# Attention scores as float32r pairs in the two halves of the TensorE array, head outputs kept transposed and collected by DMA, and convolutions of the un-normalised residual sum

## What is computed

```python
x = x + _L0_conv_ref(_gn(x), ...)   # attention, 8 heads of 16 channels
x = x + _L1_conv_ref(_gn(x), ...)   # 7x7 depthwise convolution, layer norm, MLP
# _gn: group norm, 32 groups of 4 channels, over all pixels
# attention, per image and head g (W and b per head, 16x16):
q, k, v = W x + b;  attn = softmax(q.T k * 16**-0.5);  out = v attn.T;  out = Wp out + bp
# second block:
y = conv7x7_depthwise(x) + conv_b
y = (y - mean_c(y)) * rsqrt(var_c(y) + 1e-6) * ln_g + ln_b
y = gelu(y w1 + b1) w2 + b2         # hidden width 512
```

## Time and profile before

| | |
|---|---|
| median of 3 runs | 368.73 us (368.45 to 372.86) |
| the profiled execution | 367.55 us, its span 365.6 us |
| PE busy | 309.8 us (85%) |
| DVE busy | 258.9 us (71%) |
| ACT busy | 194.1 us (53%) |
| POOL busy | 103.9 us (28%) |
| mean granted TensorE clock | 0.925 of full speed |

### The profile page before, as it was taken

The page is one execution under the profiler, slowest core; times in us unless marked ns, Lnnn a source line. Parts: engine busy times, 40 slices in busy tenths (PEclk is TensorE's granted clock), DMA queues, the critical chain, the costliest instruction groups (busy, mean ns, idle before and its releaser), DMA issues.

```text
span 365.6 us, 5601 instructions
## 1 busy us (share of the span) xinstructions
PE 309.8 (85%) x2046; PEld 106.8 (29%) x2046; DVE 258.9 (71%) x270; ACT 194.1 (53%) x359; POOL 103.9 (28%) x137
## 2 busy tenths in 40 slices
PE   7568779999990599999989999998981999698796
PEld 2244123333320133333323333333220344222242
DVE  3746759898970177887748988879898146999820
ACT  1406347767760267767757666766760546453132
POOL 5000051111010011011000036999980100894410
PEclk9969699999995599999999999999995799969899
DMA  5168950000699300000000000590000001960001
GB/s 198 29 210 129 162 104 3 30 31 0 125 120 125 37 1 2 1 2 3 1 2 0 2 2 3 158 204 5 1 2 0 0 0 74 192 167 2 0 0 57
DMA packets 11022, 19.97 MB, mean 55 GB/s; under 512 B 2035, under 2 KB 2931, under 8 KB 10995
## 3 DMA queue, kind: packets, MB, share of 16 engines
q1 hardware_dynamic: 10998, 19.64, 26.6%
HBM read 13.61 MB, written 5.54 MB: 52 GB/s over the span
## 4 chain that ended last, share of the span: by engine, by line
PE 59%; DVE 20%; DMA 9%; issue 4%; SPq 3%; ACT 2%; POOL 2%; DVEq 0%; ACTq 0%; POOLq 0%
PE ps L971 15%; PE ps L930 15%; PE ps L960 12%; DVE qs L744 11%; DMA qs<-mrows 6%; PE ps L1122 4%; DVE mx L696 4%; DMA ks<-parts_dram 2%; PE ps L1136 2%; SPq L331 2%; PE ps L951 2%; PE ps L1081 2%; PE ps L876 2%; PE ps L902 1%; ACT pr L568 1%
## 5 line engine op out<-in xcount | busy, mean ns | idle before, releaser
L696 DVE TENSOR_REDUCE mx<-ps 128x1 f32<-128x1024 f32 x128 | 154.3, 1221 | 55.5 <-PE ps L930 51.0
L568 ACT ACTIVATE pr<-ps 128x512 f32<-128x512 f32 x256 | 139.0, 595 | 98.8 <-PE ps L960 98.7
L960 PE MATMUL ps<-qs,ks 99*128 99x512 bf16 x256 | 79.6, 389 | 17.8 <-DMA qs<-mrows 16.9
L930 PE MATMUL ps<-ks,qs 96*128 96x512 bf16 x256 | 79.4, 395 | 10.7 <-DMA ks<-part 5.5
L971 PE MATMUL ps<-pr,va 128*32 128x256 f32 x1024 | 83.5, 398 | 0.0
L744 DVE SCALAR_TENSOR_TENSOR qs<-xpad,w,qs 128x512 f32<-128x512 f32 (+1 forms) x35 | 54.7, 1562 | 1.0
L433 POOL TENSOR_TENSOR mparts<-zeros,mx 128x8 bf16<-128x8 f32 x16 | 3.7, 230 | 169.0 <-DVE mx L696 169.0
L960 PEld LDWEIGHTS ps<-qs,ks 99*128 99x128 bf16 x256 | 24.5, 99 | 61.2 <-DMA qs<-mrows 16.7
L971 PEld LDWEIGHTS ps<-pr,va 128*32 128x32 f32 x1024 | 20.3, 109 | 51.4 <-issue 46.8
L930 PEld LDWEIGHTS ps<-ks,qs 96*128 96x128 bf16 x256 | 17.0, 99 | 55.5 <-issue 44.2
L1056 PE MATMUL ps<-xr,wt 128*32 128x512 f32 x224 | 30.0, 664 | 3.5 <-DMA xr<-pad_dram 3.5
...
## 6 DMA issues: line engine op xcount, KB each, us to landing
...
```

The costliest lines, as they stand in the source:

```text
L568: nc.scalar.activation(pr[:, j % PR, c * HALF:(c + 1) * HALF], st[c], ACT.Exp, scale=SCALE).then_inc(exp_done, 1)
L696: nc.vector.tensor_reduce(mx[:, r, i:i + 1], sm[i % 2], AX.X, ALU.max).then_inc(max_done, 1)
L930: last = nc.tensor.matmul(sm[i % 2][:, c * HALF:(c + 1) * HALF], qs[0:STACK, bass.ds(s * N + i * P, P)], ks[0:STACK, bass.ds(s * N + c * H ...
L960: nc.tensor.matmul(st[c], ks[0:ROWS, bass.ds(t * N + j * P, P)], qs[0:ROWS, bass.ds(t * N + c * HALF, HALF)], start=True, stop=True).then_ ...
```

## The change

Five things change together.

1. **Scores in float32r.** q and k are kept in `hl` as a float32r part and the rest (PARTS = 2), and a stack has three products: 3 x 16 = 48 rows, or 50 with the maxima. A stack lies in rows 0 to 49 or 64 to 113 of `qs` and `ks`, by heads in turn (`rows_of`: heads 0, 1, 4, 5, 8, 9, 12, 13 below, the others above), so that a score matmul uses half the rows of the array (the built program gives each a tile of 64 x 128). `qs` and `ks` have three cells of 1024 columns, which are reused; `stack` fills one head with six DMAs of 16 partitions x 1024, SBUF to SBUF, three to four heads ahead, behind that head's `row_max` in SP's queue. Nothing of the attention goes through DRAM.
2. **Order and banks.** The transposed scores, the turned maxima and denominators and some small results share the banks 4, 5 and 7 in rotation (`uses_of_banks`, `free`). `both_scores` puts one matmul of `scores_t` and one of `scores` in turn. `times_v` comes for two tiles at a time.
3. **Outputs stay transposed.** `denominators` spreads the sums over the partitions with one matmul (128 x 256), ACT copies that (`copy_turned`), and DVE takes a reciprocal of 128 x 256 and multiplies 128 x 256 (`normalise`). `collect` puts a head's output in `oc` with four DMAs. There is no turning back after heads 7 and 15; head 15 is projected from `on` with a weight of its own (`wlast`).
4. **Convolution before the norm.** `xpad` holds x1 itself (image 0's is copied by POOL, `pad_image`; image 1's is written by `residual_padded`, which replaces L837 and L298). The taps run over it, and `conv_sum` scales the sum by the group's 1/deviation and adds a `border` term, the shift times the sum of the taps inside the image, which POOL builds in `taps_inside`.
5. **Shares of the taps.** Image 0: PE 25 (7 runs), DVE 12, POOL 12. Image 1: PE 32 (9 runs), DVE 17, none on POOL or ACT. Image 1's `xr` is filled from `xpad` directly with 2 x 16 DMAs (`fill_directly`). PE's `keep_busy` matmuls before the first scores grow from 4 to 27, with eight more between the first scores, and the six behind `mlp_down(0)` are gone.

The core of the diff:

```diff
-PARTS = 3
-STACK = 6 * D
+PARTS = 2
+TERMS = 3
+STACK = TERMS * D
 ROWS = STACK + PARTS
-
-Q_ORDER = (0, 1, 2, 0, 1, 0)
-K_ORDER = (0, 0, 0, 1, 1, 2)
+GROUP_ROWS = 64
+CELLS = 3
+
+Q_ORDER = (0, 0, 1)
+K_ORDER = (0, 1, 0)
...
-PE_RUNS = (6, 8)
-DVE_TAPS = (14, 12)
+PE_RUNS = (7, 9)
+DVE_TAPS = (12, 17)
 PE_TAPS = tuple(n // SPAN * KS + n % SPAN * SHIFTS for n in PE_RUNS)
 PE_ROWS = tuple(-(-n // SPAN) for n in PE_RUNS)
-ALONE = 8
-POOL_TAPS = tuple(KS * KS - PE_TAPS[b] - DVE_TAPS[b] for b in range(B))
...
+AHEAD = 2 * NT - 3
+LATER = 2
+UT_AT = 128
+GN_AT = 384
+TURN_AT = 4
+BANKS = (4, 5, 7)
+LAST = (HEADS - 1) * D
+FINISH = {(HEADS + 1, 0): ("proj", 0), (HEADS + 1, 2): ("proj", 1), (T - 2, 5): ("mean",), (T - 1, 0): ("var",)}
...
+def uses_of_banks():
+
+    uses = []
+    for n in range(T * NT):
+        t, j = divmod(n, NT)
+        uses += [("half", n, c) for c in range(2)]
+        if j == TURN_AT:
+            uses.append(("turn", t))
+        if (t, j) in FINISH:
+            uses.append(FINISH[t, j])
+    return uses
+
+
+def rows_of(t):
+
+    return t // 2 % 2 * GROUP_ROWS
+
+
+def cell_of(t):
+
+    return (t // 4 * 2 + t % 2) % CELLS * N
+
...
+        def stack(queue, i, t, n):
+
+            order, dst = ((Q_ORDER, qs), (K_ORDER, ks))[i]
+            queue.wait_ge(S(f"part{i}{n}", t // HEADS), 2 - t // HEADS)
+            h = t % HEADS
+            for g in range(TERMS):
+                if order[g] == n:
+                    queue.dma_start(
+                        dst[rows_of(t) + g * D:rows_of(t) + (g + 1) * D, cell_of(t):cell_of(t) + N].bitcast(F32),
+                        hl[h * D:(h + 1) * D, t // HEADS, i, n, :].bitcast(F32)).then_inc(S("stack", t), 16)
+
...
+            def fill_directly(b, h):
+
+                lo, hi = ends(b, h)
+                sp.wait_ge(S("xpad", b), h + 1)
+                if h == 0:
+                    sp.wait_ge(S("conv0", b - 1), 1)
+                    sp.wait_ge(S("conv1", b - 1), 1)
+                for s in range(SHIFTS):
+                    for g in range(GROUPS):
+                        sp.dma_start(xr[s * CG:(s + 1) * CG, g, lo:hi], xpad[g * CG:(g + 1) * CG, lo + s:hi + s])\
                             .then_inc(S(f"rep{h}", b), 16)
...
+            def collect(t):
+
+                b, h = divmod(t, HEADS)
+                sp.wait_ge(ot_done, t + 1)
+                for q in range(4):
+                    sp.dma_start(oc[h * D:(h + 1) * D, b, 2 * P * q:2 * P * (q + 1)], on[q * VW:q * VW + D, t % 2, :])\
+                        .then_inc(S("collected", t % 2), 16)
+
...
+            for t in range(1, T):
+                row_max(t)
+                if t >= 2:
+                    collect(t - 2)
+                if t + 3 < T:
+                    next_stack(t + 3)
+                if t == T - 5:
+                    send_pad(0, 0)
+                    send_pad(0, 1)
+                elif t == T - 4:
+                    fill(0, 0)
+                elif t == T - 3:
+                    fill(0, 1)
+            collect(T - 2)
+            for h in range(2):
+                fill_directly(1, h)
             for k, (b, lo, hi) in enumerate(OUTPUTS):
...
+                high, low = (mparts[:, r, n * NT:(n + 1) * NT] for n in range(PARTS))
+                nc.gpsimd.tensor_copy(high, mx[:, r, :]).then_inc(m_step, 1)
+                g.wait_ge(m_step, 2 * s + 1)
+                nc.gpsimd.tensor_tensor(low, mx[:, r, :], high, ALU.subtract).then_inc(m_step, 1)
...
+            def pad_image():
+
+                g.wait_ge(S("xpad0"), 1)
+                g.wait_ge(S("x1", 0), 2)
+                nc.gpsimd.tensor_copy(inner, image(x1[:, 0, :])).then_inc(S("xpad", 0), 2)
...
+            def normalise(t):
+                r = t % 2
+                if t < T - 2:
+                    v.wait_ge(us_ready, t + 1)
+                else:
+                    v.wait_ge(ot_ready, t + 1)
+                if t >= 2:
+                    v.wait_ge(S("collected", r), 64 * (t // 2))
+                nc.vector.reciprocal(rden[:, r, :], den_of(t)).then_inc(rd_ready, 1)
                 v.wait_ge(rd_ready, t + 1)
...
+            def border(b):
+
+                v.wait_ge(S("gn_shift"), b + 1)
+                v.wait_ge(S("inside"), 2 * KS)
+                if b:
+                    v.wait_ge(S("scale"), 1)
+                nc.vector.tensor_scalar(diag[:, :], inside[:, :], nshift[:, b:b + 1], vec(V_CB), ALU.mult, ALU.add)\
+                    .then_inc(S("border"), 1)
...
             def conv_sum(k):
 
                 b, lo, hi = PIECES[k]
+                rs = gn_tiles[B + b][5][:, 0:1]
                 v.wait_ge(S("dve_tap", b), DVE_TAPS[b] * (k - b + 1))
-                v.wait_ge(S("pool_tap", b), (POOL_TAPS[b] - b) * (k - b + 1))
-                nc.vector.tensor_tensor(acc[b][:, lo:hi], acc[b][:, lo:hi], acc_pool[:, lo:hi], ALU.add)\
-                    .then_inc(S("acc"), 1)
-                v.wait_ge(S("acc"), k + 1)
+                if b == 0:
+                    v.wait_ge(S("pool_tap"), POOL_TAPS)
+                    nc.vector.tensor_tensor(acc[0], acc[0], acc_pool, ALU.add).then_inc(S("acc"), 1)
+                    v.wait_ge(S("acc"), 1)
+                v.wait_ge(S("border"), b + 1)
+                nc.vector.scalar_tensor_tensor(out=acc[b][:, lo:hi], in0=acc[b][:, lo:hi], scalar=rs, in1=diag[:, lo:hi],
+                                               op0=ALU.mult, op1=ALU.add).then_inc(S("scaled"), 1)
+                v.wait_ge(S("scaled"), k + 1)
                 v.wait_ge(S(f"conv{lo // HALF}", b), 1)
                 v.wait_ge(S(f"conv{hi // HALF - 1}", b), 1)
-                nc.vector.tensor_tensor(y[b][:, lo:hi], conv_out[:, lo:hi], acc[b][:, lo:hi], ALU.add)\
-                    .then_inc(S("y"), 1)
+                nc.vector.scalar_tensor_tensor(out=y[b][:, lo:hi], in0=conv_out[:, lo:hi], scalar=rs, in1=acc[b][:, lo:hi],
+                                               op0=ALU.mult, op1=ALU.add).then_inc(S("y"), 1)
...
+            def residual_padded(c):
+
+                lo, hi = (0, SPLIT[1] * SIDE) if c == 0 else (SPLIT[1] * SIDE, N)
+                if c == 0:
+                    v.wait_ge(S("pool_tap"), POOL_TAPS)
+                    v.wait_ge(S("dve_tap", 0), DVE_TAPS[0])
+                    for h in range(2):
+                        v.wait_ge(S(f"pad_sent{h}", 0), 16)
+                    v.wait_ge(S("projp", 1), 4)
+                nc.vector.scalar_tensor_tensor(out=inner[:, lo // SIDE:hi // SIDE, :], in0=image(lower[:, lo:hi]),
+                                               scalar=bout[:, 0:1], in1=image(xs[:, 1, lo:hi]),
+                                               op0=ALU.add, op1=ALU.add).then_inc(S("xpad", 1), 1)
...
+            def denominators(t):
                 t_.wait_ge(u_ready, t + 1)
-                t_.wait_ge(mt_done, min(t + 2, T))
-                if t == FINISH + 1:
-                    t_.wait_ge(S("gn_ve"), B + 1)
-                if later(t, 1):
-                    t_.wait_ge(ot_done, t)
-                for i in range(2):
-                    last = nc.tensor.transpose(mi[:, OT_AT + i * P:OT_AT + (i + 1) * P],
-                                               u[:, r, i * P:(i + 1) * P], ident)
-                last.then_inc(ot_ready, 1)
-
-            def scores_t(t, j):
-
-                for c in range(2):
-                    if not (isinstance(t, int) and 2 * NT * t + 2 * j + c < 2):
-                        t_.wait_ge(exp_done, 2 * NT * t + (2 * j + c - 1))
-                    nc.tensor.matmul(st[c], ks[0:ROWS, bass.ds(t * N + j * P, P)],
-                                     qs[0:ROWS, bass.ds(t * N + c * HALF, HALF)],
-                                     start=True, stop=True).then_inc(st_ready, 1)
-
-            def times_v(t, r, j):
-
-                if j == 0:
-                    if later(t, 1):
-                        t_.wait_ge(u_ready, t)
-                t_.wait_ge(exp_done, 2 * NT * t + (2 * j + 2))
+                t_.wait_ge(S("spread"), 1)
+                nc.tensor.matmul(ut_of(t), spread[:, :], u[:, t % 2, :], start=True, stop=True).then_inc(ot_ready, 1)
+
+            def scores_t(n, c):
+
+                t, j = divmod(n, NT)
+                free("half", n, c)
+                if j == 0 and c == 0:
+                    t_.wait_ge(s_mrow[t % 2], 16 * (t // 2 + 1))
+                rows = slice(rows_of(t), rows_of(t) + ROWS)
+                nc.tensor.matmul(bank("half", n, c), ks[rows, cell_of(t) + j * P:cell_of(t) + (j + 1) * P],
+                                 qs[rows, cell_of(t) + c * HALF:cell_of(t) + (c + 1) * HALF],
+                                 start=True, stop=True).then_inc(st_ready, 1)
+
...
+            def both_scores(n):
+
+                for c in range(2):
+                    scores_t(n, c)
+                    if n + AHEAD < NT * T:
+                        scores(n + AHEAD, c)
+
+            def head(t, also=()):
...
+                    n = NT * t + j
```

(78 more changed lines are left out.)

815 lines of the change are left out of this document (354 added, 461 removed).

## The result

The changed kernel takes **350.34 us** (median of 4, 349.09 to 351.01) against 368.59 of before (366.83 to 372.86). The ratio is 0.952, 95% interval 0.947 to 0.956. It is faster, by 18 us where I forecast 60, and outside my range of 287 to 328. The profiled execution took 350.4, its span is 348.6. Executions of the experiments' kernels spread by up to 5% with the granted clock (those of `e5` by 26%), so their times stand with the lowest and highest, and for `e1`, `e2`, `e4` and `e5` there is no ratio.

The account below looks back on a forecast made before the run. The bound was to move from PE to DVE in the heads; 17 + 16 + (14 x 12.0 + 1.5) + 47 + 36 + 20.8 = 306.3 us of span, so 308 us, range 287 to 328.

Parts of the forecast that it names:

- Float32r and row halves: Score matmuls: float32r costs 0.22 us per 512 columns, different row halves run side by side; `times_v` for two tiles 1.1.
- The reciprocal: DVE's `normalise`: a reciprocal of 256 columns takes 1.6 us; rival of 0.46, time 290, chance 0.2.
- The plain head: Heads 0 to 13: 12.0 us each, from DVE's 11.2 plus 0.5 and 0.3 for couplings; 12.6 before.
- serial halves: Rival for score matmuls: row halves don't overlap, or float32r needs two passes; head about 13.2, time 325, chance 0.18.
- POOL stays "under" the head: POOL in the heads: three taps and `split_max` take 11.0 us a head and stay under the head's time.
- The multiply at 0.42: DVE's `normalise`: the multiply of 256 columns is bounded by the copy of 256, 0.42 us.
- Head 9's projection at 1.5 us: Head 9: the projection and two residual halves add 1.5 us to the heads.
- the rest, 0.03: Remaining cases, chance 0.03: a slower clock while PE idles, or the start or the tail off by 10.
- The start: Before the first head: scores start about 17 us (21.3 before), first maxima take 16 (20.7 before).
- Heads 14 and 15: Heads 14, 15 to image 1's x1: 47 us (55.2 before); image 0's sum ready at 31, PE waits some 4.
- Image 1 and the tail: Image 1's convolution to its first normalised half takes 36 us (41.9 before), the tail behind it 20.8 as before.
- DMA in the way: Rival: `row_max` of the next head queues behind `collect` and `next_stack`; 2 us a head, time 336, chance 0.08.

Follow-up runs that it names:

- e5: Changed kernel with all heads in one row half (rows 0 to 49 of four cells), so no two score matmuls share the array: 389.2 us (381.1 to 480.6).
- e1: Changed kernel with the seven whole-image additions of POOL's `taps_inside` spread, one behind each `split_max` of later heads: 344.4 us (337.6 to 351.9).
- e2: Changed kernel with each half of DVE's residual sum in head 9 one reduction earlier: 344.3 us (338.9 to 354.7).
- e4: Changed kernel with DVE's reciprocal on 8 of its 256 columns, the other factors staying 1: 340.2 us (330.9 to 345.9).
- e7: Changed kernel with the edits of e1, e2 and e3 together: 328.5 us (325.1 to 331.1), 0.893 of before.
- e3: Changed kernel with POOL holding back the second tap's addition in each `conv_taps` call until DVE has multiplied: 342.4 us (339.7 to 344.9), 0.924 of before.
- e8: e7 with image 0's projection and PE's first matmul of its convolution sum (`centre_out`) each one tile later: 323.2 us (321.9 to 325.7), 0.875 of before.
- e10: e8 with four more DVE reciprocals of 128 x 256 (7.0 us, result unused) before the multiply in head 6: 331.8 us (329.4 to 335.3).

## Why the prediction missed

The miss in the span is 348.6 - 306.3 = 42.3 us. (By its own terms, 1.95 around the span and 1.2 to the median, the forecast should have read 309.4; it left the 1.2 out.) Point by point:

- **Float32r and row halves: right.** 0.235 per 512 columns against 0.22, pairs together, `times_v` 1.0 against 1.1. That tiles work independently, as the Trainium skill's "TensorEngine Tiling (Array Packing)", Tiling Modes, has it, agrees with the common starts at 152.41 and 152.74.
- **The reciprocal: right.** 1.75 against 1.6. The estimate of 2.1, from the repeat count of 8 in the Trainium skill's "VectorE: DVE Perf Modes", Walkthrough, and 1.05 ns a cycle, is too high; the measurement decides.
- **The plain head: nearly right**, 12.23 against 12.0: 14 x 0.23 = 3.2 us. The rival "serial halves" had the right mechanism: `e5` gives 0.8 a plain head where I had 1.2.
- **POOL stays "under" the head: wrong, one of the three largest steps.** I costed POOL's three taps a head and left `taps_inside` out of its queue, although the text of the change names it. 13.64 + 4.88 us of additions stand in front of a `split_max` in a head of 12.2. 8.4 us (`e1`, `e7`).
- **The multiply at 0.42: wrong beside POOL.** I had seen that DVE's taps take more beside POOL's additions and priced that for the convolution alone. 2.13 + 1.26 + 0.94 more for three multiplies, 8.5 us for the three heads with the low clock behind them (`e3` for heads 10 and 11; in head 12, 1.2 long, PE waits 0.90 for the reduction behind the multiply, read from the trace alone). The Trainium skill's "GPSIMD Engine Reference", Specifications, has the SBUF interfaces shared with VectorE, with contention for DVE instructions in a 2-port mode or with two SBUF inputs. The trace agrees: the multiply is of that kind, the reciprocal (one input) stays at 1.75 beside POOL's instructions at 188.85, 206.83 and 220.66. I had overlooked this rule.
- **Head 9's projection at 1.5 us: wrong.** It costs 8.9 over heads 8 and 9. I added instruction times and did not follow the rotation of banks round to who frees the next one (`e2`, `e8`).
- **No term for the clock: wrong.** It came under "the rest, 0.03". The heads ran at 0.90. Behind the waits of the changed kernel the clock stood at its lower level for 3.4 to 13.6 us. It is in the terms above, and 1.2 us are in head 0, which starts at a low clock (0.56 from 40 to 50): from the first transposed scores to its `u` it takes 16.0, and 12.6 in `e7`, where the clock is full. How much of `e7`'s gain is clock and how much is waits I did not separate.
- **The start: 6.6 us too long.** Scores could not start at 17: ACT issues the stacks of head 0 from 14.62, one in 0.73 us, and these 64 KB land after 3.4, where I had 1.94 from smaller ones. In the first maxima PE, not DVE, sets the pace: float32 projections of 1.1 between scores make a tile 1.74 against DVE's 1.15, and DVE waits 0.5 each time.
- **Heads 14 and 15: 8.0 too long.** The sum of image 0 was ready 33.7 us into head 14 (forecast 31); PE came to it at 30.5 (forecast 26.5), so the wait was 3.24 where I had 4, two errors that cancel. But x1 came 21.3 behind it, not 16: half clock after the wait. `e8`, without it, has 48.8 for the stage (forecast 47).
- **Image 1 and the tail: right.** Nine taps of 512 columns take 7.05, 0.78 each; 35.8 against 36, 20.2 against 20.8.
- **DMA in the way: right to be small here**, no wait for `mrows` above 1 us in the changed kernel; where the heads before it are shorter there is one in head 12, of 1.05 in `e3`, 1.15 in `e8` and 1.92 in `e10`. In `e10` the multiply of head 12 takes 0.42, and the head is still 14.7.

These add up: start 6.6, heads 3.2 + 8.4 + 7.4 (8.9 less 1.5) + 8.5 + 1.2 = 28.7 of 28.5, heads 14 and 15 8.0, the last two -0.8.

What stays open: why the clock was low so often in heads 12 to 14 of `e1`'s profiled execution (mean 0.912, 0.937 to 0.954 in the three others), and why the clock is low at head 0 in some kernels, where PE had been busy 9.60 of the 10 us from 30 (first `u` at 55.6 here, at 56.6 in `e8`, at 51.6 in `e7`). So not every fall of the clock is explained by a gap of PE.
